# Context for the convolution turned on VectorE instead of TensorE, with the engines' sequences laid out anew

## The reference

```
x = _layernorm(x + attention(x, w_q, w_k, w_v, w_o, gate, M, z))
x = _layernorm(x + xattn(ctx, ctx, x, ssm_kernel, D, 8))
x = _layernorm(x + ffn(x, gate_up_packed, gate_up_scales, down_packed, down_scales))
```

```
kv = jnp.einsum('bhil,bhjl->bijhl', k_, v_)          # 32 heads of 8 rows, l = 0..511
y = jnp.fft.irfft(kv_f * kernel_f, n=fft_size)[..., :L]   # causal convolution over l
out = y + kv * D[None, None, None, :, None]
out = jnp.einsum('bijhl,bhil->bjhl', out, q_)
```

## Time and profile before

| | |
|---|---|
| median of 3 runs | 537.16 us (536.99 to 537.49) |
| profiled execution, its span | 535.3 us |
| TensorE busy | 508.7 us, 95% of the span |
| ACT, POOL, DVE busy | 415.7, 394.7, 374.4 us |
| 64 flips of context, one each | 273 ns |
| DMA packets | 66146, of them 37882 under 512 bytes |

### The profile page before, as it was taken

One profiled execution on the slowest core, in us unless ns is written; L12 is line 12 of the kernel. 1 busy time (PEld: TensorE's weight loads), 2 busy tenths in 40 slices (PEclk: granted clock), 3 DMA queues, 4 the chain that ended last, 5 costly groups with the idle time before them and its releaser, 6 DMA issues.

```text
span 535.3 us, 11768 instructions
## 1 busy us (share of the span) xinstructions
PE 508.7 (95%) x3676; PEld 377.6 (71%) x3676; DVE 374.4 (70%) x1145; ACT 415.7 (78%) x994; POOL 394.7 (74%) x449
## 2 busy tenths in 40 slices
...
GB/s 224 203 39 63 169 142 180 128 80 99 87 112 24 159 127 86 23 100 79 60 1 117 59 59 0 118 59 59 13 130 14 39 33 49 0 1 42 1 21 39
DMA packets 66146, 40.63 MB, mean 76 GB/s; under 512 B 37882, under 2 KB 55418, under 8 KB 66106
## 3 DMA queue, kind: packets, MB, share of 16 engines
...
...
## 4 chain that ended last, share of the span: by engine, by line
PE 36%; POOL 27%; issue 19%; ACT 5%; DVE 4%; SPq 4%; DMA 2%; POOLq 1%; DVEq 0%; ACTq 0%
POOL shared L297 9%; POOL h_lo L1102 5%; SPq L415 4%; POOL kv L197 3%; PE p_cv L137 3%; PE p_cv L139 3%; PE p_cv L138 3%; PE p_n L1299 3%; PE p_n L1297 3%; PE p_n L1298 3%; POOL shared L299 2%; PE p_x L1284 2%; PE p_x L1286 2%; PE p_qk L1284 2%; PE p_qk L1286 2%
## 5 line engine op out<-in xcount | busy, mean ns | idle before, releaser
L1102 POOL TENSOR_TENSOR h_lo<-w,h_hi 128x256 f16<-128x256 f32 x88 | 73.6, 842 | 44.6 <-ACT h_hi L1151 43.0
L137 PE MATMUL p_cv<-kv_hi,toe 128*128 128x288 f16 x320 | 91.6, 286 | 1.3 <-DVE shared L257 1.3
L139 PE MATMUL p_cv<-kv_hi,toe 128*128 128x288 f16 x320 | 91.5, 286 | 0.0
L138 PE MATMUL p_cv<-kv_lo,toe 128*128 128x288 f16 x320 | 91.5, 286 | 0.0
L1134 ACT ACTIVATE p_qk<-p_qk,rescale 128x256 f32<-128x256 f32 x192 | 78.3, 451 | 12.5 <-PE p_qk L1286 11.9
L297 POOL TENSOR_TENSOR shared<-shared 128x1024 f32<-128x1024 f32 x32 | 76.8, 2399 | 8.9 <-DVE shared L257 8.8
L1134 ACT ACTIVATE p_x<-p_x,rescale 128x256 f32<-128x256 f32 x192 | 78.4, 452 | 6.2 <-PE p_x L1286 6.0
L1134 ACT ACTIVATE p_s<-p_s,rescale 128x256 f32<-128x256 f32 x144 | 59.0, 456 | 11.2 <-PE p_s L1286 11.1
L1297 PE MATMUL p_n<-wd_hi,h_hi 128*128 128x512 f16 x176 | 66.8, 379 | 0.0
L1298 PE MATMUL p_n<-wd_lo,h_hi 128*128 128x512 f16 x176 | 66.7, 379 | 0.0
L1299 PE MATMUL p_n<-wd_hi,h_lo 128*128 128x512 f16 x176 | 66.7, 379 | 0.0
...
## 6 DMA issues: line engine op xcount, KB each, us to landing
...
```

The costliest lines, as they stand in the source:

```text
L137: nc.tensor.matmul(dst, hi, kh, start=(mb == 0), stop=False)
L138: nc.tensor.matmul(dst, hi, kl, start=False, stop=False)
L139: done = nc.tensor.matmul(dst, lo, kh, start=False, stop=(mb == lb))
L1102: nc.gpsimd.tensor_tensor(h_lo[:, i, :], h32[:, i % 2, :], h_hi[:, i, :], ALU.subtract).then_inc(h_low, 1)
```

## The change

Context comes differently. For each group and each quarter k of l (128 long) there are four DMAs, one for each 32 elements of l: piece f' = 3-f of the source goes to partitions 32f to 32f+31, and each piece is 32 elements, 128 bytes. DVE then transposes 32x32 blocks and reads each backwards, so that blocks, partitions and elements together give the reversed, turned context. It writes straight into kT, which now holds all four heads in one buffer. The reversed copy, the flips on TensorE and the PSUM copies are gone. A pair product now waits for both halves of its group, and a turn waits for all pair products of the group before.

```diff
-        self.cnat = [sb(f"cnat{p}", [P, D], F32) for p in range(2)]
-        self.crev = sb("crev", [P, D], F32)
-        self.kT = [sb(f"kT{p}", [P, 2 * LB * 64], F32) for p in range(2)]
+        self.cnat = sb("cnat", [P, B, KD, 32], F32)
+        self.kT = sb("kT", [P, HG * 256], F32)
...
-    def flip_ctx(g, p):
-        pe.wait_ge(cv.ctx_reversed, g * 2 + p + 1)
-        bank_free(f"ct{p}", g)
-        for k in range(LB):
-            done = flip(cv.p_ct[:, k * P:(k + 1) * P], cv.crev[:, (LB - 1 - k) * P:(LB - k) * P])
-        done.then_inc(cv.ctx_flipped, 1)
...
-    def keep_kT(g, p):
-
-        act.wait_ge(cv.ctx_flipped, g * 2 + p + 1)
-        wait(act, cv.kv_made, (g - 1) * HG + 2 * p + 2)
-        nc.scalar.copy(cv.kT[p][:].rearrange("p (e r j) -> p e r j", e=2, j=8),
-                       cv.p_ct[:].rearrange("p (r e j) -> p e r j", e=2, j=8)).then_inc(cv.kT_kept, 1)
-
-    def reverse_ctx(g, p):
-
-        act.wait_ge(cv.in_ctx[p], (g + 1) * 16)
-        wait(act, cv.ctx_flipped, g * 2 + p)
-        src = cv.cnat[p][:]
-        nc.scalar.copy(cv.crev[:], bass.AP(src.tensor, src.offset + D - 1, [list(src.ap[0]), [-1, D]])).then_inc(
-            cv.ctx_reversed, 1)
...
-    K = cv.kT[h // 2][:, 256 * (h % 2):256 * (h % 2) + 256]
-    engine.wait_ge(cv.kT_kept, g * 2 + h // 2 + 1)
+    K = cv.kT[:, 256 * h:256 * h + 256]
+    engine.wait_ge(cv.kT_kept, g * 2 + 2)
...
+    def turn_k(g, p):
+
+        dve.wait_ge(cv.in_ctx[p], (g + 1) * 128)
+        wait(dve, cv.kv_made, g * HG)
+        c = cv.cnat[:]
+        turned = bass.AP(c.tensor, c.offset + 64 * p + 31, [list(c.ap[0]), [32, 2], [P, B], [-1, 32]])
+        nc.vector.transpose(cv.kT[:].rearrange("p (h r j) -> p r h j", h=HG, j=8)[:, 16 * p:16 * p + 16],
+                            turned).then_inc(cv.kT_kept, 1)
...
-        def load_ctx(g, p):
-            sp.dma_start(cv.cnat[p][:], ctx_in[:, g * 32 + p * 16:g * 32 + p * 16 + 16, :]).then_inc(
-                cv.in_ctx[p], 16)
+        def load_ctx(g, k):
+            c = ctx_in[:, g * 32:g * 32 + 32, :].rearrange("b s (k f c) -> k f s b c", f=4, c=32)
+            for f in range(4):
+                sp.dma_start(cv.cnat[32 * f:32 * f + 32, :, k, :], c[k, 3 - f]).then_inc(cv.in_ctx[k // 2], 16)
...
-        for p in range(2):
-            load_ctx(0, p)
         load_x(2)
...
             elif name == "cx":
-                sp.wait_ge(cv.ctx_reversed, i - 1)
-                load_ctx(g, p)
+                if i >= 4:
+                    sp.wait_ge(cv.kT_kept, 2 * (i // 4) - 1 + i % 4 // 2)
+                load_ctx(i // 4, i % 4)
...
                 if nxt and ctx:
-                    sp.wait_ge(cv.ctx_reversed, it * 2 + 2 + p + 1)
-                    load_ctx(it + 2, p)
+                    sp.wait_ge(cv.kT_kept, it * 2 + 2 + p + 1)
+                    for k in range(2 * p, 2 * p + 2):
+                        load_ctx(it + 2, k)
...
+            wait(act, deviated, 2 * i)
...
+            wait(dve, fin_made[t], f)
...
-    START_SYNC = ("x3 x4 cx2 st0 cx3 tw0 x5 st1 st2 x6 st3 toe0 xq0 xq2 toe1 xq1 x7 cx5 cx4 xr1 xr0 toe2 st4 cx6 xq3 "
...
+    START_SYNC = ("x4 cx2 x3 cx0 cx1 cx3 cx6 cx7 st0 x5 tw0 cx4 toe0 st1 x6 st2 st3 xq0 xr0 xq1 x7 xr1 toe1 "
...
-                "g8_2 y0_2 g9_0 y0_3 g10_0 g8_3 g9_1 y0_4 g10_1 g9_2 d0 rt1 y0_5 g10_2 g9_3 y0_6 d1 g10_3 xt0 y0_7 "
-                "y0_8 y0_9 xt1 y0_10").split()
...
+                "g9_3 g10_3 xt0 y0_6 y0_7 y0_8 xt1 y0_9 y0_10").split()
```

More of the change, by code:

```diff
@@ L852, in on_tensor @@
     def on_tensor(pe, flips):
-        _, flip_ctx, convolve, flip_r, flip_x2 = flips
+        _, convolve, flip_r, flip_x2 = flips
         def flip(dst, src):
@@ L1044, in on_sync, with load_ctx @@
         rows = bass.AP(toeplitz_rows.tensor, 0, [[4 * 640, 16], [1, P], [640, 4], [1, D]])
-        def load_ctx(g, p):
-            sp.dma_start(cv.cnat[p][:], ctx_in[:, bass.ds(g * 32 + p * 16, 16), :]).then_inc(cv.in_ctx[p], 16)
+        def load_ctx(g, k):
+            c = ctx_in[:, bass.ds(g * 32, 32), :].rearrange("b s (k f c) -> k f s b c", f=4, c=32)
+            for f in range(4):
+                sp.dma_start(cv.cnat[32 * f:32 * f + 32, :, k, :], c[k, 3 - f]).then_inc(cv.in_ctx[k // 2], 16)
         def load_toe(g, p):
@@ L1268, in on_tensor @@
     def on_tensor(pe, flips):
-        bank_after, flip_ctx, convolve, flip_r, flip_x2 = flips
+        bank_after, convolve, flip_r, flip_x2 = flips
         def gate_up(f, i, p):
@@ L1374, in decoder_layer @@
-    PE_ORDER = ("y1_0 g0_0 g1_0 y1_1 g0_1 y1_2 ct0 g1_1 g0_2 y1_3 y1_4 g2_0 g0_3 c2 g1_2 g3_0 c3 y1_5 g2_1 g1_3 g3_1 "
[3 rows of a table removed]
-                "y0_8 y0_9 xt1 y0_10").split()
-    DVE_ORDER = ("tm0 tm1 gu0 lk1 tm2 tm3 gu1 tm4 tm5 gu2 lk2 tm6 tm7 tm8 gu3 tm9 tm10 lk3 tm11 gu4 a1 tm12 gu5 tm13 "
-                 "kq0 tm14 tm15 b1 gu6 gu7 ln kq1 bs0 bn0 bs1 bn1 gu8 nm0 gu9 nm1 gu10 xt0 xt1 a0 b0 e1 e0").split()
-    ACT_ORDER = ("rv0 rs0_1 rs1_1 rs0_2 tl rs0_3 rs1_2 gu0 hk1 hh0 rs1_3 rs2_1 rs3_1 rs2_2 gu1 rs3_2 rs2_3 hk2 gu2 hh1 "
-                 "ct0 rs4_1 rv1 rs3_3 rs5_1 rs4_2 rs5_2 gu3 hh2 hk3 rs4_3 rs5_3 rs6_1 n1 hh3 gu4 rs6_2 ho0 gu5 hh4 "
-                 "rs7_1 hh5 kn rs6_3 rs7_2 rs8_1 ct1 rs7_3 rs8_2 gu6 gu7 rs8_3 hh6 rs9_1 rs10_1 rs9_2 ho1 rs10_2 rs9_3 "
-                 "hh7 gu8 rs10_3 gu9 hh8 gu10 hh9 xt0 hh10 xt1 n0").split()
@@ L1391, in decoder_layer @@
[L1391 to L1396 removed]
+    START_SYNC = ("x4 cx2 x3 cx0 cx1 cx3 cx6 cx7 st0 x5 tw0 cx4 toe0 st1 x6 st2 st3 xq0 xr0 xq1 x7 xr1 toe1 "
+                  "cx5 cx8 toe2 xq2 toe3 xr2 cx9 xq3 cx10 cx11 cx14 xr3 xq4 st4 cx15 xq5 cx12 toe4 toe5 cx13 "
+                  "st5 st6 st7").split()
@@ new lines, in decoder_layer @@
+    DVE_ORDER = ("tm0 tm1 tm2 lk1 tm3 gu0 gu1 gu2 tm4 tm5 tm6 lk2 tm7 tm8 kt0 gu3 gu4 tm9 tm10 gu5 kt1 lk3 "
+                 "tm11 tm12 tm13 kq0 tm14 tm15 a1 gu6 gu7 ln bs0 b1 bn0 gu8 bs1 nm0 bn1 gu9 gu10 nm1 xt0 xt1 "
+                 "kq1 a0 b0 e1 e0").split()
+    ACT_ORDER = ("rs0_1 rs1_1 rs2_1 tl rs0_2 rs1_2 hk1 rs2_2 rs0_3 rs1_3 rs2_3 gu0 gu1 gu2 hh0 hh1 hk2 rs3_1 "
+                 "rs4_1 rs5_1 hh2 rs3_2 rs4_2 rs5_2 rs3_3 rs4_3 gu3 rs5_3 gu4 hh3 rs6_1 gu5 hk3 ho0 hh4 hh5 "
+                 "rs7_1 rs8_1 rs6_2 rs7_2 rs8_2 rs6_3 rs7_3 rs8_3 n1 gu6 gu7 gu8 hh6 kn hh7 rs9_1 rs10_1 "
+                 "rs9_2 ho1 rs10_2 rs9_3 rs10_3 hh8 gu9 gu10 xt0 hh9 hh10 xt1 n0").split()
```

81 lines of the change are left out of this document (36 added, 45 removed), and 54 rows, old and new, of tables (LAST_PE, PE_ORDER, START_ACT, START_DVE).

## The result

The changed kernel takes 552.8 us (median of 4 runs, 552.52 to 553.06) against 537.33 us before (4 runs, 536.99 to 537.98): ratio 1.029, 95% interval 1.0275 to 1.0304. It is slower by 15.5 us where 532.5 (525.5 to 538.5) was predicted. The profiled execution has a span of 550.9 us against 535.3.

What follows compares the result with a forecast made beforehand. TensorE's issue was taken to bound the steady loop. Span 535.3 - 6.1 (steady) + 1.6 (start) - 0.2 (earlier last store) = 530.6; the median stands 1.86 above, so 532.5 us, range 525.5 to 538.5.

Steps and rivals of the forecast that it cites:

- 0.2 us a period of new holes: TensorE, steady periods: gate tiles in threes wait for three ACT rescalings, costing 1.2 us in all.
- Rival B: Steady periods: no change, the freed 0.86 us a period turns into waits in the new order; 537.8 us, chance 0.14.
- the prediction's own signs of being wrong: Periods near 51 us with TensorE idle at gate or convolution steps; first gate matmul past 134 or before 125; late query blocks.
- The loop is bound by TensorE's issue, with 0.5 us idle.: Steady loop of the kernel before: TensorE's matmuls and flips fill 50.7 of 51.2 us a period.
- -5.2 us, 48 flips of 0.108.: TensorE, six steady stretches: removing 48 flips at 0.108 us each saves 5.2 us, 0.86 a period.
- The hole closes, 2.1 us.: TensorE at a period's turn: a moved down step fills the 0.34 us hole, 0.3 us in each of seven turns.
- DVE turns 0.70 each, wait 0.5.: DVE: two context transposes a period at 0.70 us, plus a 0.5 us wait for POOL, covered by convolution steps in flight.
- SyncE and 128-byte pieces hidden.: Queues: 14 more issues, 8.7 us a period, and 4.2 us of small pieces a group hide in a 51 us period.
- Start +1.6 net.: Start: ends 3.2 us later through late stores and query blocks, less 1.6 given back; bounds -2 and +8.
- Rival A: Start, SyncE between first store and query blocks: slower stores and waits, +9.2 less 1.6, +7.6 us; 538.7 us, chance 0.16.

Runs made afterwards that it cites:

- 2: Changed kernel with the step lists of the steady and last periods put back to the kernel before's, its new start kept: 541.69 us (1.0091).
- 18: Kernel before, old context path, with only POOL's second pair products, DVE's late norm and ACT's hk1 moved earlier: 536.89 us (0.9995).
- 13: 5 with half of the first additions of POOL's sums left out in the steady periods: 534.05 us (0.9934).
- 14: 5 with DVE's late norm between the x_lo passes, POOL's second pair products before its last root, hk1 before gu0's silu: 533.91 us (0.9937).
- 6: 5 with one TensorE down step (y0_9) moved behind the last flip of x2: 538.66 us (1.0027).
- 10: 5 with DVE's late norm between the x_lo passes and down step y0_9 behind the last flip of x2: 538.28 us (1.0030).
- 5: 1 with the inserted context turns, the start's hk0 and the third group's context loads moved to better places: 535.60 us (0.9973).
- 1: New context path with all step lists of the kernel before, only the steps the path needs inserted or dropped: 540.16 us (1.0056).
- 3: Changed kernel with the start's lists of the kernel before, new lists kept in the steady and last periods: 553.95 us (1.0306).
- 12: Changed kernel with half of the first additions of POOL's sums left out in the steady periods: 543.79 us (1.0116).
- 4: Changed kernel with three buffers instead of two for the fp32 hidden tile h32: 549.73 us (1.0235).
- 7: Changed kernel with c2 and c3 apart among TensorE's gate steps and DVE's second query turn kq1 between gu6 and gu7: 552.04 us (1.0269).
- 15: Changed kernel with POOL's second pair products ahead of its last root and DVE's lk1 ahead of tm1 and tm2: 572.57 us (1.0642).
- 16: 7 with the heads' chain put ahead on POOL, DVE and ACT, gate tiles still in threes: 582.28 us (1.0850).

## Why the prediction was wrong

The time is 20.3 us above the forecast. Of it 2.3 us lie in the start and the second group (+3.9 where +1.6 was forecast), 18.0 in the steady periods and what follows them (+11.7 where -6.3 was).

- **"0.2 us a period of new holes ... Bounds for this: 0 and 0.5 us a period, the present idle time doubled."** This is the step that failed. It was 3.2 us (54.27 against 51.06 in 2, which has the same path and start). The bounds were taken from TensorE's present idle time, which says nothing of an order in which other engines feed it. Its reason, three rescalings of ACT, was not the wait either: TensorE waits for the terms of the convolution, for kv_lo and for x_lo. Rival B named this place, but capped the loss at the freed 0.86 us; an order can cost far more than a change frees. Two of the prediction's own signs of being wrong came: waits at convolution steps, and a first gate matmul past 134 (134.68).
- **"The loop is bound by TensorE's issue, with 0.5 us idle."** Of the kernel before this holds: 18 starts POOL's chain early, keeps the flips, and changes nothing. What it lacked is that a second bound of nearly the same length ran beside it: POOL's chain, whose last sum precedes x_lo by 7.7 us. I read POOL's 42.89 of 51.19 us as slack. Its idle time lies in front of the two roots and of the first low part of the hidden values; from there (287.36) to the last sum it has none but the 0.7 us between its passes. Shown by 13 (less POOL work, 0.33 us) and 14 with 18 (POOL's chain early, the path's worth rises from 0.19 to 0.69 us).
- **"-5.2 us, 48 flips of 0.108."** The price of a flip was right, as a ceiling: 0.86 a period forecast, 0.69 at best, 0.19 in the old order untouched.
- **"The hole closes, 2.1 us."** Wrong sign: +0.59 us a period in 6 and +0.54 in 10, both in the old order; the changed kernel has the same wait. The down step that was moved had covered the drain of the one bank for x2, and the square waits for its end.
- **DVE turns 0.70 each, wait 0.5.** Right: 0.701 and 1.6 us in the whole run. **SyncE and 128-byte pieces hidden.** Right: a context load is issued in 0.32 (median in the loop) to 0.45 us, and 5 shows no cost.
- **Start +1.6 net.** Rival A had the right place and most of the path, but its size is near by luck: its sum was +9.2 with 1.6 given back, +7.6 net, with slower stores and a wait of the context turns that did not come; measured are +7.4 to the first gate matmul with 3.5 given back, 3.9 net. My own sum had the query blocks at +3.0 (they were at +4.7, slot 2's normalization ended at 71.0 and not 67.5) and no wait for the second load (rival A's 2 us; POOL's first sum is another 1.7 late). The 3.5 us came back in the second group. That the path isn't to blame is shown by 5 (start 126.5); what else in the new lists for the start adds to it, the stretch at the lower clock included, was not taken apart.

**Open.** That the 3.2 us a period come from the order is shown (1 to 3); what in the order is so only in part: POOL's work for 1.3 (12 against 13, with kv_lo behind it), h32's two buffers for 0.35 (4), c2, c3 and kq1 for 0.45 (7), and the down step moved behind x2's last flip for 0.54 to 0.59 if it costs there what it costs in the old order (6, 10). These may overlap and do not add up to a proof. That threes as such are the root is argued from 15 and 16, which kept them and got worse, in part by the clock, and was not tried by staggering the tiles inside the new order.
